# Batch 1's loads, K and rows drawn forward in an attention and expert kernel; K in the place of unread passes

## What is computed

```python
# x, ctx: 8 batches x 256 tokens x 256 features, float32; 16 heads of 16; masks all true in these inputs
x = x + _L0_xattn_ref(_layernorm(x), ctx, ctx, Wq, Wk, Wv, Wo, bo, mask_BxS2, mask_BxSxS2)
x = x + _L0_ffn_ref(_layernorm(x), w_gate, W1, b1, W2, b2)

# attention: q from the normalised rows, k and v from ctx
attn = einsum('nhqd,nhkd->nhqk', q, k) / sqrt(16), masked to -inf
out  = einsum('nhqk,nhkd->nhqd', softmax(attn), v), then @ Wo.T + bo

# experts: 8 of them, hidden size 1024, the best two of each token, exact gelu
gate = softmax(flat_x @ w_gate.T); cw = the two largest gates of each token, else 0
h = gelu(einsum('td,edh->teh', flat_x, W1) + b1); y = einsum('teh,ehd->ted', h, W2) + b2
out = einsum('ted,te->td', y, cw)
```

## Time and profile before

| | |
|---|---|
| time, median of 3 runs | 483.51 us (481.32 to 484.29) |
| the profiled execution | 483.19 us, of which the span of the trace is 481.9 us |
| mean granted clock of TensorE | 0.975 of full |
| busy: PE, PEld, DVE, ACT, POOL | 90%, 76%, 77%, 68%, 37% of the span |
| chain that ended last, by engine | PE 49%, DVE 19%, DMA 12%, issue 8%, ACT 6% |

### The profile page before, as it was taken

How to read it: one execution, slowest core, us unless ns; L and a number is a source line. 1 busy time by engine, 2 the same in 40 slices (tenths; PEclk the granted TensorE clock), 3 DMA queues, 4 the chain that set the end, 5 groups by cost and what they waited for, 6 DMA issues and landing times.

```text
span 481.9 us, 10169 instructions
## 1 busy us (share of the span) xinstructions
PE 435.2 (90%) x3579; PEld 368.6 (76%) x3579; DVE 369.2 (77%) x816; ACT 326.1 (68%) x523; POOL 178.8 (37%) x221
## 2 busy tenths in 40 slices
PE   5897989999998977779999889999999999998993
PEld 3555666776766744568998889999889898897983
DVE  4586786878777964676989998888787787978872
ACT  2235776777556544779797688888586878867870
POOL 5219142362446537030646244322223131313323
PEclk9998999999999987997999999999999999999998
DMA  8665845425333124672688679877788778888733
GB/s 257 222 214 137 245 149 176 161 99 186 113 128 122 39 70 162 213 301 83 164 261 264 163 232 283 232 231 221 239 234 251 230 259 246 268 272 248 245 78 37
DMA packets 44768, 93.19 MB, mean 193 GB/s; under 512 B 7134, under 2 KB 30494, under 8 KB 38828
## 3 DMA queue, kind: packets, MB, share of 16 engines
q1 hardware_dynamic: 35196, 81.17, 50.9%
q0 software_dynamic: 7152, 9.46, 9.6%
q10 hardware_dynamic: 2368, 1.88, 1.2%
HBM read 63.10 MB, written 14.32 MB: 161 GB/s over the span
## 4 chain that ended last, share of the span: by engine, by line
PE 49%; DVE 19%; DMA 12%; issue 8%; ACT 6%; SPq 2%; POOL 2%; ACTq 1%; DVEq 1%; POOLq 0%
PE bank L1478 11%; PE S L1437 10%; DMA w_in<-in_W 7%; PE bank L1544 6%; DVE nmax L1020 4%; PE S L1583 4%; PE bank L1619 3%; PE bank L1536 3%; PE bank L1519 3%; PE S L1605 2%; PE S L1450 2%; ACT Q L1195 2%; DMA xin<-in_x 2%; DMA Q<-mT 1%; DVE K L866 1%
## 5 line engine op out<-in xcount | busy, mean ns | idle before, releaser
L619 POOL DMA_INDIRECT out<-y,slot x39 | 73.5, 1884 | 159.6 <-DMA out<-y,slot 84.1
L1020 DVE TENSOR_REDUCE nmax<-S 128x4 f32<-128x1024 f32 x64 | 78.0, 1222 | 35.5 <-PE S L1583 35.2
L1437 PE MATMUL S<-xgT,Q 128*128 128x256 f32 x512 | 97.6, 290 | 7.7 <-DVE xgT L893 7.7
L1334 ACT ACTIVATE prob<-S 128x1024 f32<-128x1024 f32 x64 | 65.8, 1028 | 34.3 <-PE S L1605 31.4
L1437 PEld LDWEIGHTS S<-xgT,Q 128*128 128x128 f32 x512 | 79.9, 192 | 9.4 <-issue 5.7
L866 DVE TENSOR_TENSOR K<-w_in,Q 128x1024 fp32r<-128x1024 f32 x46 | 56.3, 1223 | 26.2 <-ACT Q L1195 26.2
L1437 PE MATMUL S<-xgT,K 128*128 128x256 f32 x256 | 73.0, 285 | 0.0
L1235 ACT ACTIVATE hf<-S,b1c 128x256 f32<-128x256 f32 x128 | 53.1, 467 | 28.5 <-PE S L1437 23.9
L1478 PE MATMUL bank<-W2p,hp 128*128 128x256 f32 x528 | 68.0, 285 | 1.8 <-DVE y L923 1.8
L1478 PEld LDWEIGHTS bank<-W2p,hp 128*128 128x128 f32 x528 | 64.6, 191 | 2.0 <-issue 2.0
L1195 ACT ACTIVATE Q<-w_in 128x1024 fp32r<-128x1024 f32 x46 | 48.2, 1049 | 11.9 <-DMA w_in<-in_W 11.8
(11 more groups left out here) (222 smaller groups left out, 816.3 us busy)
## 6 DMA issues: line engine op xcount, KB each, us to landing
w_in<-in_W SPq DMA_DIRECT2D x46, 1024.0 KB
K<-flat_k SPq DMA_DIRECT2D x24, 256.0 KB, 2.4
Q<-flat_q SPq DMA_DIRECT2D x21, 256.0 KB
xg<-lists SPq DMA_DIRECT2D x16, 265.0 KB
b_in<-in_b SPq DMA_DIRECT2D x23, 128.0 KB, 6.5
lists<-zero SPq DMA_DIRECT2D x9, 265.0 KB, 3.3
cin<-in_ctxT SPq DMA_DIRECT2D x8, 256.0 KB, 3.7
xin<-in_x SPq DMA_DIRECT2D x8, 256.0 KB, 4.1
```

Of the source, the lines that this page charges most:

```text
L619: st_y[i % 4].after(pool.indirect_dma_start(out=out, out_offset=bass.IndirectOffsetOnAxis(ap=slot[i % 4][:, t:t + 1], axis=0), in_=y[i % 2 ...
L1020: max_done.after(dve.tensor_reduce(nmax[n % 4][:, :, :, m].rearrange("p t r -> p r t"), first_scores(s)[:].rearrange("p r (t k) -> p r t k ...
L1334: exp_done.after(act.activation(prob[s % 4][:].rearrange("p r t l -> p (r t l)"), S2[:].rearrange("p r l -> p (r l)"), ACT.Exp, scale=SCALE))
L1437: ins = pe.matmul(h_bank[pair][:, u, 0:n], W1p[k][a][:, kc, m * P:(m + 1) * P], xgT[k][c][:, kc, 0:n], start=(j == 0), stop=(j == len(term ...
```

## The change

Batch 1's load, statistics, K projection, K split and stack, turning of rows and Q are written one to four steps earlier; batch 2's load, statistics, `norm1`, `residual`, K and K split one step earlier. V of batch 0 goes one step later, V of batch 1 one step earlier. Six of the twelve unread passes at step -6 and the one of step 3 go, two are added at step 5. DVE normalises batch 1 at step 0. GpSimd's V constants wait for the first scores and stand behind batch 1's `rstd`. Two subtractions on GpSimd (`weight_low`) go from steps 8 and 9 to 10 and 11.

```diff
     FIRST_FRONT = {
         0: dict(load=-16, ln1=-13, norm1=-11, residual=5, k=-11, k_split=-10, k_stack=-10, xn=-8, xT=-7, q=-7, q_split=-6,
-                q_stack=-6, mask_q=-3, v=2, v_out=3, mrep=7, mx=8),
-        1: dict(load=-5, ln1=0, norm1=1, residual=6, k=1, k_split=2, k_stack=2, xn=3, xT=4, q=4, q_split=4, q_stack=5,
-                mask_q=6, v=5, v_out=6, mrep=15, mx=16),
+                q_stack=-6, mask_q=-3, v=3, v_out=4, mrep=7, mx=8),
+        1: dict(load=-7, ln1=-2, norm1=-2, residual=6, k=-3, k_split=-2, k_stack=-1, xn=1, xT=2, q=2, q_split=3, q_stack=3,
+                mask_q=5, v=4, v_out=5, mrep=15, mx=16),
...
             for s in range(START, LAST):
                 now = due[s]
+                if s == 0:
+                    pool.wait_ge(s1_done.sem, 1)
+                    value_constants()
                 if s == 12:
                     list_constants()
-                if s in (8, 9):
-                    weight_low("kq"[s - 8])
+                if s in (10, 11):
+                    weight_low("kq"[s - 10])
...
-                    if now["norm1"] == 0:
-                        value_constants()
...
-                if s == 1:
+                if s == 0:
                     dve.wait_ge(pe_misc.sem, filled_by("xn", 0))
                     normalise(0, 1)
...
-        UNREAD = {-12: 6, -6: 12, 3: 1, 6: 2, 7: 2, 9: 1}
+        UNREAD = {-12: 6, -6: 6, 5: 2, 6: 2, 7: 2, 9: 1}
```

## The result

| | before | after |
|---|---|---|
| median of 4 runs each, taken together | 482.49 us (481.32 to 484.29) | 489.97 us (488.25 to 491.71) |
| profiled execution: span, mean granted clock | 481.9 us, 0.975 | 487.0 us, 0.961 |
| start of the first turn of the maxima | 33.25 us | 39.72 us |
| start of the second turn of the maxima | 53.70 us | 59.49 us |

The ratio of after to before is 1.0149, with a 95% interval of 1.008 to 1.0218. The change makes the kernel slower, by 7.5 us in these runs. The changed kernel was run again later (the last experiment): 1.0114, interval 1.0054 to 1.0174.

What follows compares the result with a forecast made beforehand. PE in its own order was taken to pace everything behind the first steps. 0.27 + 2.87 + 0.46 + 1.7 = 5.3 us on 483.19 gave 488.5, or 488.8 us from the median 483.51; range 485.5 to 492.

Steps and rivals of the forecast that it cites:

- Batch 0's normalising: On DVE, without GpSimd's memsets beside it: 0.74 us instead of 1.91, so PE turns batch 0's rows at 8.3, not 9.49.
- Batch 1's load and K: Load issued behind the K stack, context there at 14.4 plus one microsecond allowed; K on PE from about 15.3 to 17.3.
- ACT's K copy: On ACT, batch 1's K copy waits for DMA issues and mask copies, which end at 18.2, and ends at 18.8.
- The chain on DVE: Subtraction, statistics, maxima, normalising from 18.8 to 23.66; PE turns batch 1's rows at 23.72 instead of 23.45, +0.27 us.
- PE idle for over 5 us: Sign to look for: PE has nothing from 18.1 to 23.7, 5.6 us, ahead of the turning of batch 1's rows.
- Steps 2, 3 and V behind the turning: PE work of steps 2, 3 and batch 0's V, formerly done before batch 1's turning, now follows it: +2.87 us.
- Step 5's passes: Two new unread passes on PE at step 5, with no pause to hide them, 0.23 us each: +0.46 us.
- The late waits: PE around steps 9 to 12, batch 2 a step earlier: waits of about 1.0, 1.4, 0.5; 2.9 against 2.84, so 0.
- The clock: A second clock fall from PE's idle time ahead of batch 1's turning, lasting into the work behind it: +1.7 us.
- The rival of a long fall: Clock fall longer, or a later one near 40 us too: another 1.2 to 4 us, centred on 491 us; chance 0.20.
- Passing on one for one: Behind the first steps PE paces everything, so what those steps gain or lose reaches the end in full.
- The rival "faster": Batch 1's turning not late, if ACT's DMA issues end by about 14: 478.3 us; chance 0.08.

Runs made afterwards that it cites:

- with six passes and with twelve: Unread passes at step -6: six in the changed kernel, twelve put back in a run of it, 488.73 us against before's 482.56, ratio 1.002.
- both edits: Changed kernel, twelve unread passes at step -6, batch 1's K subtraction behind its normalising, rows, Q, V at before's steps: ratio to before 0.9915, again 0.9985.
- The filled pause: Changed kernel with twelve unread passes at step -6 and 18 more ahead of the turning of batch 1's rows: ratio to before 1.0057.
- K's low part behind: Changed kernel with twelve unread passes at step -6 and DVE's subtraction for batch 1's K behind batch 1's normalising: ratio to before 0.9977.

## Why the prediction was right, and where its steps were not

488.8 us was predicted and 489.97 measured, slower by over 1%. The forecast was before's median of three runs, 483.51, and 5.3 us. With its fourth run before's median is 482.49, so what the change cost was 7.5 us at the medians, 5.1 in the profiled spans and 5.1 when it was run again: the direction and the size hold, and the nearness of the two times is in part luck. Step by step:

- **Batch 0's normalising** without the memsets: 0.74 predicted, 0.74 measured; turning 8.3, and it is at 8.33. Right.
- **Batch 1's load and K.** K was to start at 15.3, inside 14.4 to 16.5; it started at 15.88. It was to take 1.99 us and took 3.63. I had looked for a fall of the clock only behind the long pause and not here, where PE waited 2.85 us for the context. Why K fell stays open, since it fell in some executions and not in others with six passes and with twelve. The step that failed is "K runs on PE from about 15.3 to 17.3".
- **ACT's K copy** at 18.2, held by DMA issues and masks: the masks did end at 18.11 (17.02 + 1.09), but K on PE ended at 19.51 and the copy began at 19.61, released by PE. Size right for the case of K at full clock: with K at 1.99 us (both edits, first profile) the copy began at 18.30, behind the masks.
- **The chain on DVE.** From the subtraction's start (20.23) to the normalising's end (24.78) 4.55 us; predicted 18.8 to 23.66, 4.9. The normalising beside the memsets took 1.67 and not 1.91, in the bounds. The turning is 1.39 late instead of 0.27: 1.4 us more from K's late end, and 0.3 less from here.
- **PE idle for over 5 us:** 4.67. It was to be 5.6, and is shorter because K ended later.
- **Steps 2, 3 and V behind the turning,** 2.87: measured 2.78. **Step 5's passes,** 0.46: 0.53. Both right. What I left out is the wait of 0.57 us that before had behind its turning, and which the new order hides, and small new waits of 0.2 to 0.3 us. The filled pause, which has no fall, gives 3.3 us for all of these together.
- **The late waits,** 2.9 against 2.84: measured 1.18 + 1.13 = 2.31, and the third is gone in the change, where the turning ahead of it took 1.11 us at half clock. With batch 2's part on the kernel before, where that turning took 0.66, all three were there, 1.18 + 1.13 + 0.50 = 2.81, as predicted. In the change the 0 came out as -0.5; the experiment without batch 2's part gives -0.4.
- **The clock,** +1.7 for one fall of 3 to 4 us: the trace has two falls, 3.4 and 6.8 us long. They cost 1.64 on K (1.4 of it reached the turning) and 2.1 behind the turning, 3.5 in all. This term was about half of what came. The rival of a long fall, 491, had that mechanism, and a part of it is here.
- **Passing on one for one.** 5.8 at the second turn and at the sixth, 5.1 in the span. Nearly right. From about 190 us on the shift goes between 4.6 and 8.2 us, as the falls of the two executions don't lie at the same places. But after has more time at half clock behind the first 60 us than before (20.4 against 17.0 us), not less, so the 0.7 us that are missing at the end have no cause that I can show.

So the total came out by terms that err against each other: the clock too small by some 2 us, the waits too large by 0.5 + 0.6, the chain on DVE by 0.3, and the last 0.7 given back. That they cancel is luck. The mechanism holds: the pause ahead of batch 1's turning, because DVE's chain can't start before K has gone through PE and ACT. The rival "faster" failed at that chain, as the prediction said. The prediction had it decided by the end of ACT's DMA issues; the experiments show that they hold back the turning only through the subtraction. With it moved, ACT's copy of K was no earlier (18.47), and the turning came at 21.17 all the same; PE still waited 1.87 us for it, so the case of no wait at all was not reached. The clock's part varies between executions, and with the executions taken first (ratio 1.0149) the change looked worse than later (1.0114); both lie in each other's interval.

On the port rule that the prediction weighed (the Trainium skill, GPSIMD Engine Reference, Specifications) the runs agree in kind: the same pair of instructions took 0.73 to 0.74 us with GpSimd still, 1.67 with the three memsets and the work behind them beside it, and 0.87 when the memsets had begun 1.12 us earlier and ended soon after it began. The other half of the rule, that memsets beside the maxima would cost nothing, agrees too: with K's low part behind, the maxima at 19.10 took 1.23 us with the memsets beside all of it, and 1.21 to 1.23 elsewhere.

## What to carry to other kernels

Before a projection is drawn forward, ask what its low part or copy stands in front of on the other engines: a subtraction that nobody needs yet, but which waits for PE and ACT, holds back statistics and maxima that were ready, and the pause comes out on PE several instructions later. A long pause on the engine that bounds the kernel can cost twice, once itself and once more where the clock falls behind it, and filling it with unread passes returned only the second here. And take no term of the clock from one execution: run the same kernel twice before a fall is put down to an edit. Look as well at how many executions a ratio rests on: a gain that came from five of ten was not there when the kernel was run again.

## What was not expected of the hardware

- The same kernel had the same eight matmul records at 1.99 us in one execution and 3.68 in another, with waits of 1.43 and 1.87 us ahead of them.
- Before's span over 25 executions on one chip ranges over 6.5 us, and most of it goes with the mean granted clock. A difference of 1% between two executions may be clock alone. Both edits gave 0.9915 and then 0.9985, the first from 5 of 10 executions, the second from all 12.
- The chips differ by as much as the change does: before's median was 478.5, 482.6, 485.1 and 485.4 us on four of them.
